# Eight of the in-place maxima of the attention move from VectorE to ScalarE

## What is computed

```
q = (x @ Wq.T + bq).reshape(B, M, H, dqk)      # M = 2048, H = 8, dqk = 2
k = (x @ Wk.T + bk).reshape(B, M, H, dqk)
v = (x @ Wv.T + bv).reshape(B, M, H, dv)       # dv = 16
scores = jnp.einsum('bmhd,bnhd->bhmn', q, k) / math.sqrt(dqk)
scores = jnp.where(scores >= 0, scores, 0.2 * scores)
beta = jax.nn.softmax(scores, axis=-1)
out = jnp.einsum('bhmn,bnhd->bmhd', beta, v).reshape(B, M, C)
```

```
x = x + _L0_attn_ref(_layernorm(x, axis=-1), ...)
x = x + _L0_ffn_ref(_layernorm(x, axis=-1), ...)
x = x + _L1_attn_ref(_layernorm(x, axis=-1), ...)
x = x + _L1_ffn_ref(_layernorm(x, axis=-1), ...)
```

## Time and profile before

| | us |
|---|---|
| median of 3 runs | 859.79 |
| lowest and highest of them | 858.88 and 862.38 |
| the profiled execution's own time | 859.69 |
| its span, first to last instruction | 857.6 |
| attention units in the profiled execution, first to last exponential | 46.8 to 376.5 |

### The profile page before, as it was taken

The page is one execution under the profiler, slowest core; times in us unless marked ns, Lnnn a source line. Parts: engine busy times, 40 slices in busy tenths (PEclk is TensorE's granted clock), DMA queues, the critical chain, the costliest instruction groups (busy, mean ns, idle before and its releaser), DMA issues.

```text
span 857.6 us, 18232 instructions
## 1 busy us (share of the span) xinstructions
PE 725.3 (85%) x6309; PEld 438.2 (51%) x6309; DVE 603.7 (70%) x1330; ACT 498.8 (58%) x747; POOL 424.7 (50%) x659
## 2 busy tenths in 40 slices
PE   4789999999999999961899999868587674999991
PEld 2422223222222333320899999445553522999991
DVE  5899999899999989956577754336667663444451
ACT  4778888888888878850344444534344121555550
POOL 4140002164226324677677876577677743355552
PEclk9999999999999999985899999987565756999996
DMA  8999999999999700144566665112432331233336
GB/s 254 295 294 295 310 304 298 316 301 297 313 302 331 314 2 23 39 106 130 143 165 173 171 172 149 56 53 89 132 98 87 108 113 32 40 53 52 50 46 159
DMA packets 83482, 142.96 MB, mean 167 GB/s; under 512 B 10736, under 2 KB 75728, under 8 KB 81888
## 3 DMA queue, kind: packets, MB, share of 16 engines
q1 hardware_dynamic: 57744, 118.07, 45.7%
q0 software_dynamic: 12784, 17.40, 8.6%
q10 hardware_dynamic: 12864, 6.33, 2.8%
HBM read 116.57 MB, written 101.34 MB: 254 GB/s over the span
## 4 chain that ended last, share of the span: by engine, by line
PE 66%; DVE 11%; ACT 7%; issue 5%; POOL 5%; DMA 4%; SPq 1%; POOLq 0%; DVEq 0%; ACTq 0%
PE PS L669 14%; PE PS L1015 8%; PE PS L655 8%; PE PS L644 7%; PE PS L807 4%; PE PS L794 4%; PE PS L796 4%; PE PS L1025 4%; POOL GB L1458 3%; ACT PB L1151 2%; PE PS L782 2%; ACT PB L1154 2%; PE PS L854 2%; ACT PS L1146 1%; PE PS L958 1%
## 5 line engine op out<-in xcount | busy, mean ns | idle before, releaser
L1684 DVE TENSOR_SCALAR PS<-PS 128x1024 f32<-128x1024 f32 x241 | 286.3, 1228 | 16.3 <-PE PS L644 13.0
L1151 ACT ACTIVATE PB<-PS 128x1024 f32<-128x1024 f32 x192 | 195.6, 1025 | 39.4 <-PE PS L655 33.2
L669 PE MATMUL PS<-PB,VS 128*32 128x256 f32 x2048 | 164.2, 393 | 0.1
L1398 POOL DMA_INDIRECT slots_scratch<-XN,slot x96 | 93.0, 969 | 50.6 <-ACT PB L1151 25.9
L1458 POOL DMA_INDIRECT GB<-y_scratch,slotc x96 | 91.4, 952 | 42.5 <-issue 26.9
L644 PE MATMUL PS<-QS,KP 64*128 64x512 bf16 (+1 forms) x640 | 99.1, 340 | 10.3 <-ACT PB L1151 4.0
L655 PE MATMUL PS<-QM,KP 64*128 64x512 bf16 (+1 forms) x640 | 100.2, 342 | 2.2 <-DVE PS L1684 2.1
L1488 POOL DMA_INDIRECT sums_scratch<-YO,XG x39 | 60.6, 1554 | 57.2 <-DVE YO L2039 56.0
L655 PEld LDWEIGHTS PS<-QM,KP 64*128 64x128 bf16 x640 | 25.7, 93 | 103.5 <-issue 49.9
L1015 PE MATMUL PS<-XTT,WB 128*128 128x128 f32 x624 | 75.9, 275 | 0.0
L1154 ACT ACTIVATE PB<-PS 128x1024 f32<-128x1024 f32 x64 | 64.8, 1026 | 13.8 <-PE PS L655 12.6
(11 more groups left out here) (297 smaller groups left out, 1359.4 us busy)
## 6 DMA issues: line engine op xcount, KB each, us to landing
y_scratch<-YP SPq DMA_DIRECT2D x80, 128.0 KB, 2.0
slots_scratch<-slots_scratch SPq DMA_DIRECT2D x1, 8768.0 KB
W0GU<-in_w0gu SPq DMA_DIRECT2D x1, 6144.0 KB, 48.3
XP<-slots_scratch ACTq DMA_DIRECT2D x80, 64.0 KB, 2.3
XP<-slots_scratch SPq DMA_DIRECT2D x80, 64.0 KB, 2.2
W1GU<-in_w1gu SPq DMA_DIRECT2D x8, 512.0 KB, 4.1
W0D<-in_w0d SPq DMA_DIRECT2D x1, 3072.0 KB, 17.0
XG<-slots_scratch SPq DMA_DIRECT2D x39, 68.5 KB, 1.9
```

What stands on the lines that cost most here:

```text
L669: last = mm(PS[32 * j:32 * j + 32, at:at + HALF], VS[:, n, g * HG + j, :], PB[u // 2 % 3][:, 2 * (j % 2) + j // 2, q], start=(n == 0 and h ...
L1151: A(PB[u // 2 % 3][:, 2 * hp:2 * hp + 2, :], pair_banks(u).rearrange("p (j q) -> p j q", j=2), ACT.Exp).then_inc(sem("exp_done"), 1)
L1398: gp.indirect_dma_start(slots0_dram.rearrange("b p d -> (b p) d"), bass.IndirectOffsetOnAxis(ap=slot0[:, t, k:k + 1], axis=0), XN[:, t, 0: ...
L1684: TS_(pair_banks(u), pair_banks(u), 4.0, 0.0, ALU.mult, ALU.max).then_inc(sem("relu_done"), 1)
```

## The change

A third table of places is added, and the test that decides who does the maximum takes it in for full-length rounds without routing. The places are 12 and 26, so the 13th and the 27th of 32; there are four such rounds, so eight maxima move. ScalarE's form of the operation is the one that it uses already: a Relu with scale 4, from PS to PS, 128x1024.

```diff
         ACT_RELUS = (14, 25, 27, 31)
         LATE_RELUS = (18, 21, 25)
+        PLAIN_RELUS = (12, 26)
...
         def relu_on_act(u):
 
-            return routing_place(u) in ACT_RELUS or late_place(u) in LATE_RELUS
+            plain = pair_of(u)[3] is None and routing_place(u) < 0
+            return routing_place(u) in ACT_RELUS or late_place(u) in LATE_RELUS or (plain and place_of(u) in PLAIN_RELUS)
```

## The result

The changed kernel takes 864.83 us (median of 14 runs, 862.36 to 866.55); the kernel before, on the same chips, 858.94 us (14 runs, 857.55 to 862.52). The ratio is 1.006, with an interval of 1.0047 to 1.0074. Forecast were 864.3 us and a ratio of 1.0052. The ratio's interval is 4.0 to 6.4 us of difference. Three executions of this record stood far outside (1160.58 us of the changed kernel, 1721.12 and 2069.25 of the kernel before), and all medians and ratios here leave them out.

A forecast was written before the change was run, and what follows sets the result against it. The prediction took the loop exponential, scores, values, shifted (2.40 us for two units), not VectorE, to bound plain rounds. Relief of VectorE counted 0, eight ScalarE maxima 8 x 0.56 = 4.5 us: 859.8 + 4.5 = 864.3 us, range 861.8 to 867.0.

The forecast's parts named there:

- The bound: Plain attention rounds: the closed loop exponential, scores, values, shifted takes 2.40 us for two units; VectorE is not in it.
- The price: Each maximum moved to ScalarE in a plain round costs 0.56 us, which is not made good afterwards.
- measured instance in another round: Round 2, place 14, already with a ScalarE maximum: exponentials 12 to 16 take 5.36 us against 4.80 in the plain rhythm.
- The steps of ScalarE's starts: Around each moved maximum, from exponential 10 to 14: steps of 1.86, 0.90, 1.50 and 1.11, together 5.37 us.
- The sum: Eight moved maxima in four plain rounds cost 8 x 0.56 = 4.5 us, bounds 4.0 to 4.8.
- the part behind shifts as a whole: After the attention, everything starts from the last exponentials, so the loss reaches the end unchanged.
- the granted clock as the exception: Around the first expert products: the clock's rise may come earlier or later against the later start, 2 us either way.
- My own sign for being wrong: Behind the attention: the distance from the last exponential to the end changes by over 1 us.
- VectorE as the bound: Plain rounds: VectorE limits, so relief shortens four rounds by 6.8 us in all, to 853.0 us; chance 0.05.
- Hidden: Plain rounds: ScalarE's idle time and freed VectorE absorb the maxima; 859.8 us, or 862 if half absorbed; chance 0.12.
- Full price: Plain rounds: both chains of the loop are held up, 0.80 us a maximum, 6.4 in all, 866.2 us; chance 0.08.

The follow-up runs named there:

- two orders of TensorE's list: Values split in two parts around scores, one unit later, without and with the change: by heads 992.87 and 992.22 us, by queries 908.52 and 910.89 us.
- long addition: Kernel before plus an extra 128x1024 addition on VectorE ahead of its maxima of places 12 and 26 in plain rounds: 867.97 us, plain rounds 39.95 us.
- four and one maxima: Changed kernel with other places per plain round: four (9, 14, 21, 26), 872.62 us, ratio 1.0138; one (12), 864.20 us.
- long copy: Kernel before, all maxima on VectorE, plus a 128x1024 copy into an unused tile on ScalarE at places 12 and 26: 866.87 us, ratio 1.0073.
- two short delays: Kernel before plus, at places 12 and 26, a 128x256 copy on ScalarE (862.04 us) or a 128x128 addition on VectorE (866.16 us).
- short addition: Kernel before plus a 128x128 addition on VectorE ahead of its maxima of places 12 and 26 in plain rounds: 866.16 us, plain rounds 38.54 us.

## Why the prediction was right, and where it was thin

**The bound.** The loop over exponential, scores, values and shifted is the bound of a plain round. Shown from four sides: delaying the exponential costs the same whoever does the maximum (39.66 and 39.66 us), small delays on ScalarE and VectorE are free (38.54), VectorE's relief is worth nothing, and the price falls to 0 where TensorE is the limit. The last holds for two orders of TensorE's list, in one of which half a us of delay is made good.

**The price.** Taken from a measured instance in another round, 0.56 us; measured 0.565 in rounds 1, 3 and 5. That VectorE had been doing statistics in that instance made no difference, as the starts of its maxima had said. The steps of ScalarE's starts around the place were forecast as 1.86, 0.90, 1.50 and 1.11 and came as 1.862, 0.904, 1.490 and 1.107.

**The sum.** 8 x 0.56 = 4.5 us; the attention is longer by 4.2. Rounds 1, 3 and 5 give 1.13 each. Round 0 gives 0.83 (39.69 to 40.52), because its first four steps take 5.77 us instead of 6.07, ahead of the first moved maximum. Both profiles of each kernel show it. The granted clock shows where it comes from. At the start of the attention it falls to 0.50 (1.2 GHz) for a stretch, here in the changed kernel:

```profile
47.57:50.98 3.41, 3.06 (x18) 0.54 (x16) 2.80 (x3) 2.14 (x3) 3.33 (x3) 0.50 0.97 288
```

and in the kernel before:

```profile
48.82:52.23 3.41, 3.41 (x24) 0.64 (x22) 2.66 (x3) 2.16 (x3) 3.33 (x3) 0.50 0.44 115
```

The first exponentials start at 46.23 and 46.78, so the stretch begins 1.34 us behind the first exponential in the one and 2.04 in the other. Over the ten profiles with the order of TensorE as before, the first four steps lengthen with this distance: 5.52 us at 0.53 (long addition), 5.62 and 5.65 at 1.0 and 1.1 (four and one maxima), 5.77 and 5.78 at 1.3 and 1.4 (the changed kernel), 5.91 at 1.7 (long copy), 6.07 to 6.16 at 2.0 to 2.3 (the kernel before and the two short delays). So the 0.3 us goes with the place of the low clock and not with the moved maxima. Why it fell earlier in every kernel whose plain rounds are longer was not tried.

**What was left to the range: behind the attention.** The forecast said that the part behind shifts as a whole, and named the granted clock as the exception, 2 us either way. The windows of the changed kernel answer to the earlier trace rows:

```profile
409.00:413.00 4.00, 0.00 (x0) 0.00 (x0) 0.00 (x0) 0.00 (x0) 3.31 (x13) 0.50 0.21 61
413.50:419.50 6.00, 5.87 (x27) 5.31 (x28) 1.90 (x5) 2.04 (x3) 1.46 (x5) 0.50 0.38 105
419.70:430.00 10.30, 10.30 (x95) 10.28 (x95) 7.13 (x19) 4.89 (x13) 7.92 (x26) 1.00 0.55 151
```

The expert products start at 413.5 and run at 1.2 GHz until 419.6: 6.1 us, where it was 4.3 (409.7 to 414.0). The stage of these experts, from its first transpose to the start of its last product, follows this length by and large (1.8 us more at half speed are 0.9 us of work). Where the low stretch is 4.2 to 4.3 us (both profiles of before, and the two short delays, whose attention is not longer) the stage takes 127.0 to 127.6 us. Where it is 6.1 to 6.2 us (both of the changed kernel, and the long copy) it takes 128.2 to 129.0. With four places a round the low stretch is 3.5 us and the stage 126.8. That is about 1 us (0.6 and 1.2 in the two pairs of profiles). Whether the change causes it is not shown. The long addition has an attention just as long, and its expert products begin at 413.76, 0.05 us after those of the changed kernel's second profile (413.71), yet its low stretch is 4.4 us and its stage takes 127.6:

```profile
413.76:418.10 4.34, 4.16 (x19) 3.65 (x20) 1.53 (x4) 1.67 (x2) 0.54 (x3) 0.50 0.47 128
418.20:430.00 11.80, 11.80 (x109) 11.79 (x108) 7.87 (x21) 5.65 (x15) 9.32 (x31) 1.00 0.54 143
```

So the low stretch is not set by when the products begin alone. The way there did shift as a whole, as forecast: from the end of the last exponential to the first expert product it is 33.2 to 33.5 us in all fourteen profiles.

The rest of the part behind the attention scatters without regard to the change: 483.4 and 487.1 us in the two kernels with short delays, whose attention is as long as before, against 481.1 and 481.9 in the unchanged one, and 483.5 to 485.6 in the kernels with a long one. My own sign for being wrong, a shift there by over 1 us, did show in the profiles (3.2 and 3.5 us); about 1 us of it lies in the stage of the first experts, some 2.4 us behind that stage, and what they are is not settled. With an interval of 4.0 to 6.4 us for the whole difference and 4.2 in the attention, the medians do not settle either whether the change costs anything there.

**How near the total came.** The attention accounts for 4.2 of the measured 5.9 us, and at most for that: in the changed kernel's profiles it also begins 0.5 to 0.7 us earlier, so that its end, counted from the start of the span, comes only 3.4 and 3.7 us later. The forecast put 4.5 on a median of three runs, 859.79, that was 0.85 over the median of fourteen. So that 864.3 lies so near 864.83 is in part luck; the size of the step in the plain rounds is not.

**The rivals.** VectorE as the bound (853.0) fell with the long copy: VectorE's two maxima in or out of its list, the same 39.66. By that rule, the Trainium skill's on a saturated VectorE (Perfetto Trace Analysis, Optimizing Scalar/DVE Operations), the share might have paid; the run with the short addition disagrees with calling this VectorE saturated, since 0.28 us more on it was free. The rival's own sum was off too: it took 1.065 us for each of ScalarE's operations, which start 0.90 to 0.92 us apart back to back, so ScalarE would not have become the limit at 36.8 us. Hidden: only the first 0.37 us on ScalarE is hidden. Full price (0.80 each) did not occur; 0.655 did, with odd distances, and that is a case that the prediction had not seen.

## What to carry to other kernels

An engine that is busy 98% of a stretch need not be its bound. It is not if it starts instructions on the heels of what it waits for and its own results lie ready before they are used (here 0.34 us); follow one result around until the chain closes, and compare that time with the period. Moving work from such an engine onto one that is in the closed chain costs its length less the spare time in front of the instruction that it delays (here 0.94 less 0.37 us), even if that engine is idle 14% of the time. Where the chain has slack, the same move cost nothing. If the same edit already stands elsewhere in the program, its price can be read there, from a start ahead of it to a start four steps on; here that gave 0.56 us for a measured 0.565.

## What was not expected of the hardware

- A block of values products with two heads of 32 columns takes TensorE as long as one with four: 0.56 us for 2 x 256 columns against 0.57 for 4 x 256, from the start of a block to what follows it. Halving the columns and keeping four heads brings it to 0.36 us only, so two halves cost 0.72. What follows shifted starts 0.32 us behind it when it is values and 0.23 when it is scores.
- Delays of the same length can cost different amounts by their distance: in the run with four places the rhythm of a pair (1.295 and 1.107 us) restarts with its long step after each delay, and an odd number of steps left between two of them costs 0.094 us more.
- The clock's rise does not follow the first busy moment by a fixed time: in the profiles it came 3.5 to 6.2 us after the expert products began, and 4.4 and 6.1 us in two profiles in which they began within 0.05 us of each other.
- Where a stretch of low clock falls at the start of the attention moved its first four steps between 5.52 and 6.16 us.
